# Experts pass: GpSimd issues the scatter-add of the tile behind ahead of the gather of the tile three ahead

## What is computed

```python
x = x + _L0_xattn_ref(_layernorm(x), ctx_2048, mask, ...)
x = x + _L0_ffn_ref(_layernorm(x), gate_weight, w_gate, w_up, w_down)   # 64 experts, top 8 of each token

# the experts, per token row of an expert:
g = ragged_dot(sorted_tokens, w_gate, group_sizes)     # 1024 -> 384
u = ragged_dot(sorted_tokens, w_up, group_sizes)       # 1024 -> 384
out = ragged_dot(silu(g) * u, w_down, group_sizes)     # 384 -> 1024
y = sum(outs * topk_w[:, :, None], axis=1)
```

## Time and profile before

| | |
|---|---|
| median of 3 runs | 6567.19 us (6564.72 to 6573.34) |
| profiled execution, its own time | 6554.6 us |
| its span | 6553.0 us |
| TensorE matmul busy | 6387.5 us, 97% of the span |
| TensorE weight loads busy | 5666.8 us, 86% |
| VectorE, ScalarE, GpSimd busy | 3695.7, 2889.1, 2123.3 us |
| TensorE's granted clock, mean | 0.991 of full speed |
| DMA | 1049.59 MB, 160 GB/s over the span |

### The profile page before, as it was taken

The page is one execution under the profiler, slowest core; times in us unless marked ns, Lnnn a source line. Parts: engine busy times, 40 slices in busy tenths (PEclk is TensorE's granted clock), DMA queues, the critical chain, the costliest instruction groups (busy, mean ns, idle before and its releaser), DMA issues.

```text
span 6553.0 us, 105959 instructions
## 1 busy us (share of the span) xinstructions
PE 6387.5 (97%) x31978; PEld 5666.8 (86%) x31979; DVE 3695.7 (56%) x4618; ACT 2889.1 (44%) x3319; POOL 2123.3 (32%) x1887
## 2 busy tenths in 40 slices
PE   9999998999999999879999999999999999999998
PEld 7888887887888788779989999999899999999997
DVE  5443434999999889835454454443533444444444
ACT  3222224888888744424343343332422333333333
POOL 1010000000000145544444454444444444444444
PEclk9999999999999999989999999999999999999999
DMA  8754565555555577557676776665755566666666
GB/s 281 242 193 148 149 148 145 129 130 127 128 128 126 150 195 170 137 122 196 157 215 167 187 198 168 169 169 111 193 113 111 140 140 169 143 164 168 157 160 164
DMA packets 844890, 1049.59 MB, mean 160 GB/s; under 512 B 440705, under 2 KB 638081, under 8 KB 844802
## 3 DMA queue, kind: packets, MB, share of 16 engines
q0 software_dynamic: 123984, 368.70, 25.4%
q1 hardware_dynamic: 564432, 382.50, 23.7%
q10 hardware_dynamic: 156386, 297.29, 13.3%
HBM read 725.85 MB, written 322.31 MB: 160 GB/s over the span
## 4 chain that ended last, share of the span: by engine, by line
PE 48%; DMA 3%; issue 2%; DVE 2%; POOL 1%; ACT 1%; DVEq 0%; ACTq 0%; POOLq 0%; SPq 0%
PE moe_ps_gate L1394 5%; PE moe_ps_gate L1396 5%; PE moe_ps_gate L1395 5%; PE moe_ps_up L1396 5%; PE moe_ps_up L1395 5%; PE moe_ps_up L1394 5%; PE moe_ps_y L1383 5%; PE moe_ps_y L1382 5%; PE moe_ps_y L1381 5%; PE moe_ps_hT L1401 1%; DMA moe_tokens<-h2st,moe_rows 1%; DMA first_raw<-in_w_up 1%; DVE moe_gu_lo L1502 1%; POOL moe_tokens L1336 1%; DMA out<-moe_y,moe_rec_s 1%
## 5 line engine op out<-in xcount | busy, mean ns | idle before, releaser
L1336 POOL DMA_INDIRECT moe_tokens<-h2st,moe_rows x1156 | 1256.4, 1087 | 1902.2 <-DVE moe_rows L1512 1633.8
L1394 PE MATMUL moe_ps_gate<-moe_gu_hi,moe_xT_hi 128*128 128x384 f32 x2288 | 794.2, 347 | 67.8 <-DVE moe_xT_lo L1506 51.4
L1525 DVE SCALAR_TENSOR_TENSOR moe_hidden<-moe_hidden,moe_rec_w,moe_ps_up 128x384 f32<-128x384 f32 x286 | 175.6, 614 | 1150.7 <-PE moe_ps_up L1396 963.0
L1395 PE MATMUL moe_ps_gate<-moe_gu_lo,moe_xT_hi 128*128 128x384 f32 x2288 | 767.8, 336 | 0.0
L1396 PE MATMUL moe_ps_gate<-moe_gu_hi,moe_xT_lo 128*128 128x384 f32 x2288 | 767.6, 335 | 0.0
L1394 PE MATMUL moe_ps_up<-moe_gu_hi,moe_xT_hi 128*128 128x384 f32 x2288 | 765.0, 334 | 0.6 <-DVE moe_gu_lo L1502 0.6
L1395 PE MATMUL moe_ps_up<-moe_gu_lo,moe_xT_hi 128*128 128x384 f32 x2288 | 764.6, 334 | 0.0
L1396 PE MATMUL moe_ps_up<-moe_gu_hi,moe_xT_lo 128*128 128x384 f32 x2288 | 764.5, 334 | 0.0
L1430 ACT CAST moe_xT_hi<-moe_ps_turned 128x1024 fp32r<-128x1024 f32 x287 | 291.2, 1015 | 905.0 <-PE moe_ps_up L1396 708.2
L1383 PE MATMUL moe_ps_y<-moe_d_hi,moe_hT_lo 128*128 128x512 f32 x1722 | 676.5, 393 | 0.0
L1382 PE MATMUL moe_ps_y<-moe_d_lo,moe_hT_hi 128*128 128x512 f32 x1722 | 675.0, 392 | 0.0
(11 more groups left out here) (207 smaller groups left out, 13742.0 us busy)
## 6 DMA issues: line engine op xcount, KB each, us to landing
first_raw<-in_w_gate ACTq DMA_DIRECT2D x63, 1536.0 KB
first_raw<-in_w_up ACTq DMA_DIRECT2D x63, 1536.0 KB
moe_raw_d<-in_w_down ACTq DMA_DIRECT2D x63, 1536.0 KB
proj_a_raw<-in_ctxT POOLq DMA_DIRECT2D x64, 512.0 KB, 5.7
kst<-proj_o SPq DMA_DIRECT2D x256, 128.0 KB, 2.8
vst<-proj_o SPq DMA_DIRECT2D x64, 512.0 KB, 2.6
qst<-proj_o SPq DMA_DIRECT2D x256, 128.0 KB, 2.2
att_kt<-kst SPq DMA_DIRECT2D x64, 512.0 KB
```

The lines of the kernel that those rows point to most:

```text
L1336: nc.gpsimd.indirect_dma_start(out=tokens[:, g * (H // G):(g + 1) * (H // G)], out_offset=None, in_=h2_quarters, in_offset=bass.IndirectOf ...
L1394: nc.tensor.matmul(o[:, 0:I], xT_hi[:, c], gu_hi[:, b, k, c], start=(c == 0), stop=False)
L1395: nc.tensor.matmul(o[:, 0:I], xT_hi[:, c], gu_lo[:, b, k, c], start=False, stop=False)
```

## The change

Two calls of the loop body trade places with the other two, so that in each tile's step GpSimd does `add(t-1)` and then `gather(t+3)`. No instruction, transfer or buffer is added or removed.

```diff
                 def two_tiles(h):
+                    add(h, 2 * h - 1, 1)
                     gather(2 * h + 3)
-                    add(h, 2 * h - 1, 1)
+                    add(h, 2 * h, 0)
                     gather(2 * h + 4)
-                    add(h, 2 * h, 0)
 
                 two_tiles(0)
                 with pool.Fori(1, pairs) as h:
                     two_tiles(h)
                 add(pairs, last_tile, 1)
```

## The result

| | before | after |
|---|---|---|
| median | 6569.0 us of 5 runs (6564.72 to 6573.34) | 6604.07 us of 5 runs (6599.15 to 6609.35) |
| ratio, 95% interval | | 1.0055 [1.0044, 1.0067] |
| profiled execution, its own time and span | 6554.6, 6553.0 us | 6609.35, 6607.7 us |

The changed kernel is slower by 35 us where 125 were predicted: the sign holds, the size is under a third of the forecast, and the time lies in the stated range only at its foot.

What follows compares the result with a forecast made beforehand. TensorE bounds the kernel, its matmuls busy for 97% of the span. Terms 70 + 50 + 8 - 3 = 125 us take the profiled 6554.6 us to 6680, on the median of the runs 6692 us, 1.9% slower; range 6588 to 6765.

Steps and rivals of the forecast that it cites:

- the step on which all rests: First tiles: the scatter-add's transfer holds GpSimd's DMA queue; gather lands 5.7 us later, next transpose at T'+12.5, not 6.8.
- the prediction's own sign: If the transpose behind a first tile comes by T'+10.9, time stays near 6575 and the queue's step failed.
- Issue: First tile: the scatter-add's issue on GpSimd comes first, so the last gather's issue ends 1.6 us later.
- The bound: A transpose may start 10.9 us after its step's first down matmul (T) for nothing; beyond, each us costs one.
- forecast 55 holes: Behind first tiles: some 55 TensorE stops of 1.6 us before a down matmul, released by VectorE's `hT_lo`.
- 70 us for experts of three or more tiles: 44 such experts, each losing 1.6 us to a late transpose behind the first tile; no second hole.
- 50 for those of two: 11 such experts at 4.5 us each: 1.6, as much again for `xT_lo`, 1.3 in the next first tile.
- 8 for those of one: 6 such experts at 1 to 2 us each: `y` waits for `w_up` and the gather stands behind it.
- the end -3: End of the pass: the previous scatter-add goes ahead of the last four gathers; 3 us back, of 0 to 5.
- Rival 1: The scatter-add does not hold the queue, only delays issue by 1.6 us: T'+8.4, +8 us, 6575; chance 0.13.
- Rival 2: Equal turns, or scatter-add through before weights come in force: +25 us, 6592; equal turns give T'+10.1; chance 0.13.
- plain tiles free: Plain tiles: scatter-add at T+6.9, gather at T+8.8, transpose at T'+2.5, perhaps T'+3.2; they cost nothing.

Runs made afterwards that it cites:

- e3: Changed order with half a scatter-add (only the first 512 features of each row), against before: 6593.2 us, ratio 1.0044.
- e7: Order of before with half a scatter-add (only the first 512 features of each row), against before: 6546.08 us, ratio 0.9966.
- e4: Changed order with `rec_s` loaded early, ahead of SyncE's wait for `hidden`, against before: 6579.21 us, ratio 1.0021.
- e10: Changed order with `rec_s` loaded early and `w_down` loaded later, behind ScalarE's copy of `y`, against before: 6576.77 us, ratio 1.0033.
- e12: Of each pair of tiles: gather, both scatter-adds, gather; with `rec_s` loaded early, against before: 6681.55 us, ratio 1.0194.
- e9: Order of before with `rec_s` loaded early, ahead of SyncE's wait for `hidden`, against before: 6551.6 us, ratio 0.9998.
- e1: Order of before, but each gather first waits for what the scatter-add waits for, against before: 6627.69 us, ratio 1.0094.
- e8: Only every second tile has the new order (gather, both scatter-adds, gather), against before: 6716.18 us, ratio 1.0227.

## Why the prediction was right in sign and wrong in size

**The step that failed** is the one that the text called the step on which all rests: "It starts at 5011.4 and holds the queue to about 5016.1 ... The gather of a first tile lands 5.7 us later and the transpose starts at T'+12.5 instead of 6.8." Measured: T'+10.2 in that tile. The queue's share, landing behind the end of the gather's issue, grew by 0.7 us and not by 4.1 (5.7 less the 1.6 of issue); over 34 such tiles the median grew by 0.2. And e3 and e7 show that it isn't the bytes ahead that cost. By the prediction's own sign, a transpose by T'+10.9, it is the queue's step that failed; the time did not stay near 6575 as that sign said, because the holes stand elsewhere, as below. The windows in that first tile (last two columns: DMA share, GB/s) failed their mark as well: 250 GB/s were forecast from T+11 to T+16.

```profile
5052.60:5057.60 5.00, 5.00 (x26) 4.45 (x25) 3.67 (x4) 1.01 (x1) 4.22 (x3) 1.00 1.01 291
5057.60:5065.00 7.40, 7.40 (x44) 7.16 (x43) 0.43 (x1) 1.89 (x3) 1.29 (x3) 1.00 1.05 328
```

**Issue: right in kind, too small.** I took GpSimd to wake for `y` alone, the last issue 1.6 us later. It was 2.7 us later in that tile (the last gather issued until T+17.5; T+16.5 forecast), since the scatter-add has another wait, for `rec_s`, which never ended last before, when five us of gather stood ahead of it. The code shows that wait; the sum put it at nothing without a reason. That was the avoidable slip: *every* wait of a moved instruction is added to what it is moved ahead of.

**The bound: right where stated, but the holes stand elsewhere.** Of the forecast 55 holes in front of a down matmul, released by `hT_lo`, the waits of after have 12, 14.4 us in all. Ten of them end the first tile itself, where the transpose was at T+9.9 or later. Only two, 1.0 us, stand behind the tile that the forecast meant, with its transpose at T'+11.5 and T'+11.7, which fits the bound of 10.9. The tiles behind first tiles, at T'+10.2 in the median, mostly stay under it; a dozen pass it, by up to 1.9 us, and all but these two show no such wait. I had left the bound of a first tile at "under 9.2"; it is T+7.4. The lateness made in one first tile (3.3 us in the tile shown) decays over the next tiles: in experts of three or more that follow another such, the medians of the transpose from T are, in the first tile and the three behind it, 6.8, 10.2, 6.6 and 3.8 after, against 5.9, 7.1, 3.1 and 2.6 before. If the expert ends before it is gone, the next first tile starts late and meets `w_down`. That is why a hole depends on the length of the expert *before*: those that follow one of four or more tiles have some 1 us in all (31 of them), those after three 12.5 (0.8 before), those after two 36.5 (some 9 before).

**The terms of the sum**, as holes of after less those of before: 70 us for experts of three or more tiles, measured 27; 50 for those of two, measured 10; 8 for those of one, measured 11; the end -3, measured -3.3. The 27 us are not the 1.6 us in each of 44 experts that the sum has: nearly all are holes in or right behind a first tile, and only 1.0 us stands where the sum had it. The measured terms also hold what TensorE lost at half clock, some 8 us, which the sum had no term for. The sum of holes and end is 45 us in the profiled executions, and the medians differ by 35.

**The rivals.** Rival 1 had the mechanism nearest to the truth, "it only delays the issue by 1.6 us", but its T'+8.4 and +8 us left out the wait for `rec_s`. Rival 2's T'+10.1 and +25 us are nearest in numbers, from a reason (equal turns in the queue) that e3 and e7 speak against. Of the rule weighed there, the Trainium skill's order of descriptors within one queue ("DMA: Bandwidth & Descriptors", Two DMAs through the same engine are not ordered): no run contradicts it, but in the tile shown it cost the gather no more than 0.7 us.

**Right**: plain tiles free, T+6.9, T+8.8 and T'+2.6; the tail. **Luck**: VectorE's wait for tokens at about 700 us (701.2), since the forecast had some 55 long waits of near 10 us behind first tiles, and measured are 103 waits more than before, none longer than 8.6 us. And the time is in the stated range because its foot was put at rival 2.

**Open.** 14 of the 35 us remain with the rows early. Waits for `rec_s` are still in them, and so are the wait for `y` (last for most scatter-adds of e4) and the scatter-add's own 1.6 to 2.9 us of issue; no run took the issue or the wait for `y` away, so their shares aren't known. A second `tokens` buffer wasn't tried.

## What to carry to other kernels

Before an instruction is moved ahead of another, list all that it waits for, loads of a few hundred bytes too, and read from the trace when each is *there*: a wait that never shows today may only be hidden by what stands ahead. A stage with eight us of slack in the plain case can have none in the special one, and lateness is carried over; so find the bound in each kind of tile, and ask how many tiles it takes to recover. Count a long stop of TensorE with the slow stretch behind it. Load row numbers as soon as their buffer is free, and big weights behind the small transfers that somebody waits for.

## What the runs showed of the hardware

**A 1 KB load can take three to five times as long beside large transfers.** `rec_s` lands 1.7 us after its issue in the median of after (2.4 in e10), and 5.4 and 8.8 us in the rows above. The Trainium skill ("DMA: Bandwidth & Descriptors", Latency and other measured facts) has memory latency rise from 0.2 to 2 us under high load; the trace agrees in direction, but 3.7 and 6.4 us more are beyond one such latency, and the profile doesn't say where it is spent.

**A scatter-add of 128 rows of 4 KB takes 5.9 us at the least to land and 10.9 at most** in e12 (median 6.3), of which some 3.3 us, an estimate from the earlier trace rows, are its own time on the DMA engines.

**TensorE's clock halves behind a stop and comes back.** In after it was 0.5 for 3.4 or 6.8 us at a time, six times, behind stops of 2.4 to 5.8 us, and other stops of up to 2.8 us left it at 1.00.

**TensorE's undisturbed step differs by 0.2% between executions**, whatever the order: it averages 12.78 us in those of before, e3 and e9, 12.81 in after, e1 and e8, and the other kernels lie between, at a granted clock of 1.00 in the windows shown of both orders. Over 281 steps that is 7 us of the difference between the profiled spans of before and after, and belongs to no edit. Of two single profiles, a difference of that size says nothing.
